# A vision tower in one kernel: where GpSimd makes the third low weight part of an output projection

## The reference

```python
proj = hidden_states @ W_in.T
u, gate = jnp.split(proj, 2, axis=-1)
# u: a causal convolution of 4 taps over the tokens, bias, silu
# dt, Bm, Cm from u @ Wx.T, each with an RMS norm; delta = softplus(dt @ Wdt.T + dt_bias)
def step(state, xs):
    d_t, B_t, C_t, u_t = xs
    dA = jnp.exp(d_t[..., None] * A)
    state = dA * state + (d_t * u_t)[..., None] * B_t[:, None, :]
    y_t = jnp.einsum('bdn,bn->bd', state, C_t)
    return (state, y_t)
# y = all y_t + u * D_param;  y = y * silu(gate);  return y @ W_out.T
```

## Time and profile before

| | |
|---|---|
| median of 3 runs | 3937.91 us |
| lowest, highest | 3933.69, 3937.98 us |
| the profiled execution's own time | 3936.17 us |
| its span (first to last instruction) | 3934.4 us |
| mean granted TensorE clock | 0.99 of full speed |
| TensorE matmul busy | 3778.9 us, 96% |
| VectorE busy | 2639.2 us, 67% |
| ScalarE busy | 2037.1 us, 52% |
| GpSimd busy | 2178.9 us, 55% |

### The profile page before, as it was taken

How to read it: one execution, slowest core, us unless ns; L and a number is a source line. 1 busy time by engine, 2 the same in 40 slices (tenths; PEclk the granted TensorE clock), 3 DMA queues, 4 the chain that set the end, 5 groups by cost and what they waited for, 6 DMA issues and landing times.

```text
span 3934.4 us, 67770 instructions
## 1 busy us (share of the span) xinstructions
PE 3778.9 (96%) x27088; PEld 2534.3 (64%) x27088; DVE 2639.2 (67%) x2979; ACT 2037.1 (52%) x2986; POOL 2178.9 (55%) x932
## 2 busy tenths in 40 slices
PE   5889999999999999999999999999999999999999
PEld 1567787444777777544577877744477777754467
DVE  7965572999446573699736565499935557289963
ACT  7742354887332343778533233588723234388742
POOL 0024443999534343799743434499943343389962
PEclk7999999999999999999999999999999999999999
DMA  5242334000322223200133223400032223410022
GB/s 126 77 145 81 91 113 158 20 17 16 121 94 89 81 94 137 98 14 19 64 114 98 81 85 119 151 13 20 24 128 97 86 86 113 153 38 20 13 87 80
DMA packets 97164, 320.76 MB, mean 82 GB/s; under 512 B 12401, under 2 KB 16753, under 8 KB 92401
## 3 DMA queue, kind: packets, MB, share of 16 engines
q1 hardware_dynamic: 80752, 275.70, 21.9%
q10 hardware_dynamic: 16128, 41.03, 3.1%
HBM read 272.51 MB, written 44.17 MB: 80 GB/s over the span
## 4 chain that ended last, share of the span: by engine, by line
PE 61%; DVE 20%; issue 15%; ACT 4%; POOL 0%; ACTq 0%; DVEq 0%; POOLq 0%
PE psg L999 45%; DVE sb_wst L1860 18%; PE psg L1037 3%; ACT sb_dA L809 2%; PE psx L1249 2%; PE psg L1043 1%; PE psx L1322 1%; PE psg L1300 1%; PE psx L1016 1%; DVE sb_du L1843 1%; PE psg L1404 1%; PE psg L1307 1%; ACT sb_yh L911 1%; PE psg L1426 1%; PE psg L1147 1%
## 5 line engine op out<-in xcount | busy, mean ns | idle before, releaser
L543 POOL TENSOR_TENSOR sb_wl<-sb_raw,sb_wh 128x1024 fp32r<-128x1024 f32 x388 | 954.3, 2463 | 1661.5 <-ACT sb_wh L660 1661.4
L1860 DVE TENSOR_TENSOR_SCAN sb_wst<-sb_dA,psx 128x1024 f32<-128x1024 f32 x512 | 1130.0, 2266 | 2.8 <-PE psx L1249 2.8
L660 ACT ACTIVATE sb_wh<-sb_raw 128x1024 fp32r<-128x1024 f32 x388 | 408.8, 1056 | 666.7 <-PE psg L999 429.6
L809 ACT ACTIVATE sb_dA<-sb_dlt,sb_a_sb 128x504 f32<-128x504 f32 x1024 | 647.2, 705 | 63.8 <-DVE sb_wst L1860 61.9
L1249 PE MATMUL psx<-sb_dgB,sb_duT 64*64 64x256 f32 x8192 | 576.0, 388 | 52.3 <-DVE sb_wst L1860 48.5
L578 POOL TENSOR_TENSOR sb_wst<-sb_wst,sb_cb_lo 128x1024 f32<-128x1024 f32 x256 | 600.3, 2370 | 35.5 <-DVE sb_wst L1860 35.5
L1249 PEld LDWEIGHTS psx<-sb_dgB,sb_duT 64*64 64x64 f32 x8192 | 291.0, 133 | 485.6 <-DVE sb_wst L1860 342.7
L1270 PE MATMUL psg<-sb_wst,sb_cst 64*64 64x512 f32 x4096 | 591.3, 593 | 2.2 <-ACT sb_twin L800 1.6
L578 POOL TENSOR_TENSOR sb_wst<-sb_wst,sb_cb_hi 128x1024 f32<-128x1024 f32 x248 | 578.9, 2368 | 7.1 <-DVE sb_wst L1860 6.9
L999 PE MATMUL psg<-sb_xh,sb_wh 128*128 128x512 f32 x2080 | 533.3, 398 | 4.6 <-POOL sb_wl L543 2.1
L999 PE MATMUL psg<-sb_xh,sb_wl 128*128 128x512 f32 x2080 | 515.5, 390 | 0.0
(11 more groups left out here) (293 smaller groups left out, 4929.7 us busy)
## 6 DMA issues: line engine op xcount, KB each, us to landing
sb_raw<-in_w SPq DMA_DIRECT2D x360, 512.0 KB, 3.5
sb_raw<-w_ffn_dequantized SPq DMA_DIRECT2D x32, 512.0 KB, 3.3
gates<-sb_gt ACTq DMA_DIRECT2D x64, 256.0 KB, 2.1
sb_gin<-gates SPq DMA_DIRECT2D x64, 256.0 KB, 2.7
h_after_tok<-sb_h SPq DMA_DIRECT2D x4, 2048.0 KB, 8.7
sb_cb_lo<-c_rows ACTq DMA_DIRECT2D x8, 1024.0 KB, 5.4
sb_cb_hi<-c_rows ACTq DMA_DIRECT2D x8, 1024.0 KB, 5.6
sb_h<-h_after_tok SPq DMA_DIRECT2D x4, 2048.0 KB, 7.9
```

The lines of the kernel that those rows point to most:

```text
L543: pool.tensor_tensor(rest(b, i0), raw[:, i0 % RAW, :, :], high(b, i0).bitcast(F32), ALU.subtract).then_inc(s_wl, 1)
L660: A(high(b, i0), raw[:, i0 % RAW, :, :], ACT.Copy).then_inc(s_wh, 1)
L809: ins_ = A(dA[:, (m * NQ + k) % RING, :, n, 1:S], dlt[:, m % 2, :].rearrange("p (b s) -> p b s", b=NB)[:, :, 1:S], ACT.Exp, scale=a_sb[:, ...
L1860: v.tensor_tensor_scan(wst[:, x, 4 * j:4 * j + 4, :, :].rearrange("p b n s -> p (b n s)"), dA[:, x, 4 * j:4 * j + 4, :, :].rearrange("p b ...
```

## The change

GpSimd makes the low parts of W0 and W1 ahead of the scan stage, as before. The low part of W2 moves from there to behind GpSimd's last gate product, directly ahead of the low part of W3. ScalarE's list (the constant `AHEAD` stays 3), SP's list, TensorE's and VectorE's are as they were; so is the number of instructions.

```diff
@@ the GpSimd program, in each of the four blocks
                 if stop >= 4:
                     split_loop(b, WIN0, 8)
-                    splits(b, WOUT0, WOUT0 + AHEAD)
+                    splits(b, WOUT0, WOUT0 + 2)
                     pool.wait_ge(s_cb, 16 * NQ * (b + 1))
...
                     pool.wait_ge(s_pd, (b + 1) * TAIL)
                     gated(DC - 2)
-                    splits(b, WOUT0 + AHEAD, WOUT0 + 4)
+                    splits(b, WOUT0 + 2, WOUT0 + 4)
                     split_loop(b, WOUT0 + 4, 3)
```

## The result

| | median | lowest to highest | runs |
|---|---|---|---|
| before | 3936.01 us | 3933.69 to 3938.0 | 14 |
| changed | 3944.44 us | 3942.76 to 3946.82 | 14 |

The ratio is 1.0022, 95% interval 1.0015 to 1.0029: the change makes the kernel 8.4 us slower, against 8.6 forecast. The forecast time was 3946.5 us and the measured one is 3944.44; of the 2.1 us between them 1.9 are the starting point, since the prediction began from the median of three runs, 3937.91, and the 14 runs of before here have 3936.01. The profiled execution's span went from 3934.4 to 3941.3 us.

A forecast was written before the change was run, and what follows sets the result against it. The prediction took TensorE, busy 96% of the span, as the bound, with VectorE's queue at the tail leaving it no slack. Four blocks at 2.16 us add 8.6 to 3937.9, giving 3946.5 us; range 3939 to 3950.

The forecast's parts named there:

- The front gives nothing: Front of each block's scan stage: removing GpSimd's 2.40 us low part of W2 there gains 0.
- The tail costs 2.16 us per block: Tail: GpSimd's added W2 operation stops VectorE, so gated product m=15 and TensorE's k=15 come 2.16 us later.
- The low parts and loads are covered: Output projection: W2 and W3 low parts are ready over 5 us before TensorE's reads; W4's load costs 0.
- Nothing behind gives it back: Behind the tail: TensorE's matmuls run without a gap into the strips, so the 2.16 us delay is kept whole.
- Rival (a): Tail: GpSimd's 1.68 us idle gap hides the operation, 3937.9 us, or 3940.8 if partly hidden; chance 0.14.
- Rival (b): Tail: VectorE is stopped for longer, 2.4 to 2.9 us per block, 3947.5 to 3949.5 us; chance 0.22.
- Rival (c): Front: W2's low part delayed the first scan or product; with the tail hidden, 3928.3 us; chance 0.03.
- (d): GpSimd's queue: the change does not do what it says; same time as rival (a); chance 0.01.

The follow-up runs named there:

- front-only run: Kernel before, with GpSimd's front low part of W2 cut to its first eighth and nothing added at the tail; 3936.79 us, ratio 1.0003.
- the two with the gate product first: VectorE's gate product m=15 put behind the fourth low part of y instead of the eighth: in the changed kernel 1.0002, in the kernel before 1.0003.
- W2 and W3 behind it: Changed kernel, with GpSimd waiting for VectorE's gate product m=15 before making the low parts of W2 and W3; 3934.82 us, ratio 0.9999.
- tail only: Changed kernel, with W2's low part also made at the front, uncounted, and made again at the tail; 3943.79 us, ratio 1.0020.
- memset: Changed kernel, with a GpSimd memset of W2's low-part slot, which only writes SBUF, ahead of W2's low part; 3943.95 us, ratio 1.0019.
- quarters: Changed kernel, with W2's low part made at the tail in four GpSimd operations of 128x256 each; 3944.83 us, ratio 1.0023.
- W2 made twice: Changed kernel, with W2's low part made twice in a row at the tail, the second waiting for the first; 3963.50 us, ratio 1.0069.

## Why the prediction was right

1. *The front gives nothing.* Shown by the front-only run: 1.0003 (0.9994 to 1.0012), with seven eighths of the operation gone.
2. *The tail costs 2.16 us per block.* Measured 2.23 us to L1849 (10.30 - 8.07) and 2.20 us "to W4" (21.60 - 19.40), in all four blocks. The order of events was as worked out: gate product, one L1925, W2, one L1925, W3; W2 and W3 end 0.9 and 1.0 us earlier than I wrote, 0.83 of it because this execution's scan started that much earlier. The term is 0.04 to 0.07 us small, because both weight operations now stop VectorE for 2.19 to 2.20 us (2.88 - 0.68 and 2.87 - 0.68). The prediction's reason for taking 2.16 and not 2.40, that the waiting operation's own dispatch overlaps the stop, isn't shown. The sizes show 0.2 us per GpSimd operation that stop nobody, and don't tell whose time they are. Four tails make 4 x 2.20 = 8.8 us, the medians 8.4.
3. *The low parts and loads are covered.* GpSimd ends at 1010.96, TensorE needs W3 at about 1019.5; SP issues W4's load at 1008.4. Moving both 5 us later cost nothing that the runs can tell.
4. *Nothing behind gives it back.* "To W4" keeps all of it, and so does the next block: from tail to tail the changed kernel takes 925.0 us, before 922.7 (the next point has the one longer distance).
5. *The span grew by 6.9 us, not 8.6.* 0.83 us of the difference come from ahead of the first scan. Another 1.0 us is in the profile of before itself: from the second tail to the third it takes 923.8 us (2850.91 - 1927.10), from the first to the second 922.7 and from the third to the fourth 922.8; in the changed kernel all three are 925.0. The granted clock of that execution of before between 2530 and 2550 is 0.83, of the changed one 1.00 (columns: busy us of PE, PEld, DVE, ACT, POOL, then clock, DMA share, GB/s; first before, then changed, whose third scan stage starts 3.8 us later, so that only the clock is to be compared):

```profile
2530.00:2550.00 20.00, 16.90 (x138) 9.46 (x138) 13.53 (x10) 16.32 (x24) 13.62 (x7) 0.83 0.21 70
```

```profile
2530.00:2550.00 20.00, 15.96 (x129) 10.20 (x127) 10.74 (x8) 16.75 (x24) 8.63 (x4) 1.00 0.17 57
```

Two spans of one execution each would have given the wrong size; the distances inside the stage gave the right one. This dip isn't an accident of one execution. All five profiled kernels without the added wait (before, front only, the two with the gate product first, W2 and W3 behind it) have a granted clock of 0.83 over the first 20 us of the third scan stage, where the other four have 0.91 or 1.00, and take 923.8 or 923.9 us from the second tail to the third; four of them, all but before, take 924.4 to 925.1 from the third to the fourth. The four with one added wait of 2.2 us (changed, tail only, memset, quarters) take 925.0 both times. So in these executions the kernels without the wait lose up to 3 us more outside the tails, at the lower clock as far as the rows tell. Why, and whether other executions do the same, isn't shown; the 0.4 us between 8.8 and 8.4 stay open.

Rival (a), the idle gap hides it, is refuted: the gap did hide the operation on GpSimd and it cost the full price on VectorE. Rival (b), a stop of 2.4 to 2.9 us per block, is refuted by the tails' 2.20 us: VectorE gets in between W2 and W3. Rival (c), a gain at the front, is refuted by the front-only run, and the timelines answer (d). The sum of 9.6 us from the rule of the Trainium skill ("SBUF — State Buffer", "Who interferes with whom"), the whole 2.40 us of the instruction, is 0.8 us above what the tails show, and the measurement decides; its kind of stop and the exemption of a writer are as the runs have them.

## What to carry to other kernels

In this kernel an idle stretch on GpSimd was free at the front and cost its full price at the tail. Before filling such a stretch, ask whether a VectorE operation with two SBUF inputs stands on or near the critical path beside it; look there for VectorE operations that are long by just GpSimd's duration. Cutting the GpSimd operation in four didn't help. Putting the critical VectorE result ahead of the stops, or the GpSimd work behind it, brought the time back to that of before, within the interval.

## What was not expected of the hardware

A wait of TensorE can cost more than its length. After 4.3 us (W2 made twice) its clock fell to the lower level in each of the four tails, 1.6 to 2.1 us on top. After 2.2 us (the changed kernel's profile) it did not fall in any. Of the 12 tails of the tail-only, memset and quarters profiles, which have the same wait, it fell in two, the first of tail-only and the first of memset, and those tails are 1.5 us longer. The clock there from TensorE's restart to W4's high part (tail-only, columns as above):

```profile
1016.61:1028.07 11.46, 11.46 (x44) 9.34 (x45) 4.58 (x8) 0.00 (x1) 0.00 (x0) 0.86 0.01 1
```

Why the same wait of 2.2 us lowers the clock in two of 16 tails and not in the others isn't shown. Waits between the two lengths weren't tried.
